# Gates of a graph layer: the two sums of a pair of units stand together, and the three parts of a pair are picked and passed through the sigmoid in another order

## What is computed

```python
hg = jnp.einsum('bnf,gf->bng', h3, Wg[:, :F])
qg = jnp.einsum('blf,gf->blg', q, Wg[:, F:]) + bg
attn = jax.nn.sigmoid(hg[:, :, None, :] + qg[:, None, :, :])
qi = jnp.einsum('bnlf,blf->bnf', attn, q)
```

## Time and profile before

| | |
|---|---|
| median of three runs | 1491.56 us (1490.84 to 1495.92) |
| span of the profiled execution | 1493.6 us |
| TensorE busy | 1374.3 us (92%) |
| VectorE busy | 992.7 us (66%) |
| ScalarE busy | 773.0 us (52%) |
| GpSimd busy | 225.7 us (15%) |
| pairs of the first gate | 155.3 to 275.1 us of the span |
| pairs of the second gate | 375.6 to 495.6 us |

### The profile page before, as it was taken

How to read it: one execution, slowest core, us unless ns; L and a number is a source line. 1 busy time by engine, 2 the same in 40 slices (tenths; PEclk the granted TensorE clock), 3 DMA queues, 4 the chain that set the end, 5 groups by cost and what they waited for, 6 DMA issues and landing times.

```text
span 1493.6 us, 24053 instructions
## 1 busy us (share of the span) xinstructions
PE 1374.3 (92%) x10000; PEld 1165.3 (78%) x10000; DVE 992.7 (66%) x1776; ACT 773.0 (52%) x1245; POOL 225.7 (15%) x115
## 2 busy tenths in 40 slices
PE   6999999999999798798789999888999999987998
PEld 5999633699533696588778899778899999976976
DVE  8655777745777756657667677776577767758355
ACT  2346788535788444344554454634345554436343
POOL 4201587100677100102001000001000000000100
PEclk8999999999999899999999899899899999988899
DMA  8174464135364222035324354063355555142100
GB/s 341 45 231 159 127 190 118 64 127 168 119 190 117 75 78 103 0 128 186 111 81 185 127 191 149 22 234 118 115 184 188 171 191 182 61 170 80 69 0 22
DMA packets 30834, 194.81 MB, mean 130 GB/s; under 512 B 4211, under 2 KB 4339, under 8 KB 14726
## 3 DMA queue, kind: packets, MB, share of 16 engines
q1 hardware_dynamic: 30726, 193.27, 38.1%
HBM read 183.03 MB, written 3.93 MB: 125 GB/s over the span
## 4 chain that ended last, share of the span: by engine, by line
PE 73%; DVE 15%; ACT 6%; POOL 3%; issue 1%; DMA 1%; SPq 0%; DVEq 0%; ACTq 0%; POOLq 0%
PE PS L357 58%; PE PS L956 6%; PE PS L965 5%; PE PS L362 3%; DVE WL L300 2%; POOL WK L1151 2%; PE PS L609 1%; PE PS L459 1%; POOL WL L307 1%; DVE SM L534 1%; ACT WH L293 1%; DVE SM L1323 1%; ACT WK L1708 1%; DVE WK L1733 1%; DVE WK L1738 1%
## 5 line engine op out<-in xcount | busy, mean ns | idle before, releaser
L300 DVE TENSOR_TENSOR WL<-w,WH 128x768 fp32r<-128x768 f32 x367 | 349.5, 963 | 216.1 <-ACT WH L293 213.5
L293 ACT ACTIVATE WH<-w 128x768 fp32r<-128x768 f32 x381 | 315.9, 841 | 272.3 <-PE PS L357 264.2
L357 PE MATMUL PS<-XS,WH 128*128 128x256 f32 x2292 | 418.5, 285 | 11.5 <-DVE XS L484 7.1
L357 PEld LDWEIGHTS PS<-XS,WH 128*128 128x128 f32 x2292 | 356.4, 190 | 15.7 <-issue 12.0
L357 PE MATMUL PS<-XS,WL 128*128 128x256 f32 x1146 | 324.2, 283 | 0.0
L357 PEld LDWEIGHTS PS<-XS,WL 128*128 128x128 f32 x1146 | 217.9, 190 | 0.0
L1089 DVE TENSOR_TENSOR WK<-PS,WK 128x1024 f32<-128x1024 f32 x128 | 156.7, 1224 | 55.6 <-ACT PS L1033 54.5
L1151 POOL TENSOR_TENSOR WK<-WK 128x1024 f32<-128x1024 f32 x64 | 152.8, 2392 | 205.7 <-ACT WK L1030 205.7
L357 PE MATMUL PS<-WH,GS 128*128 128x256 f32 x864 | 162.4, 286 | 6.8 <-DVE GS L484 6.7
L1033 ACT ACTIVATE PS<-PS 128x1024 f32<-128x1024 f32 x128 | 129.4, 1011 | 34.8 <-PE PS L956 34.8
L357 PEld LDWEIGHTS PS<-WH,GS 128*128 128x128 f32 x864 | 137.2, 192 | 9.7 <-DVE GS L484 8.1
(11 more groups left out here) (249 smaller groups left out, 2059.1 us busy)
## 6 DMA issues: line engine op xcount, KB each, us to landing
w<-f2W_in SPq DMA_DIRECT2D x40, 1152.0 KB, 5.5
w<-Wrel_in SPq DMA_DIRECT2D x12, 1152.0 KB, 9.0
WK<-qrep_in SPq DMA_DIRECT2D x16, 768.0 KB, 5.4
w<-f1Wi_in SPq DMA_DIRECT2D x8, 1152.0 KB, 5.9
w<-f1Wo_in SPq DMA_DIRECT2D x8, 1152.0 KB, 5.1
w<-f3Wqkv_in SPq DMA_DIRECT2D x6, 1152.0 KB, 13.8
RT<-qg_rows SPq DMA_DIRECT2D x16, 384.0 KB, 6.3
RT<-AS SPq DMA_DIRECT2D x32, 192.0 KB, 6.6
```

What stands on the lines that cost most here:

```text
L293: A.e.activation(w_hi(i), w_raw(i), ACT.Copy).then_inc(*hi("w", i))
L300: V.e.tensor_tensor(w_lo(i), w_raw(i), w_hi(i), ALU.subtract).then_inc(*lo("w", i))
L357: ins = T.e.matmul(o, l, r, start=i == 0 and first, stop=i == n - 1 and last, skip_group_check=lint)
```

## The change

In TensorE's loop the picks of a round are no longer those of one pair. A round p now has `select(p, 1)`, `select(p-1, 2)`, both sums of pair p-2, and then `select(p, 0)`; six picking matmuls stand in a row across the end of a round, then 16 summing ones (in the trace's count). `turn_q` stays the last thing of its round, which now puts it behind `select(p, 0)`. ScalarE takes the parts in the order 1, 0, 2. Nothing is added or taken away.

```diff
             T.wait_ge(act, "pick")
             gate_q(0)
             gate_q(1)
+            select(0, 1)
             select(0, 0)
-            select(0, 1)
             gate_q(2)
             select(0, 2)
             gate_q(3)
+            select(1, 1)
             select(1, 0)
-            select(1, 1)
             gate_q(4)
-            select(1, 2)
             gate_q(5)
             for p in range(2, NPR):
+                select(p, 1)
+                select(p - 1, 2)
+                sums(p - 2, 0)
+                sums(p - 2, 1)
                 select(p, 0)
-                select(p, 1)
-                sums(p - 2, 0)
-                select(p, 2)
-                sums(p - 2, 1)
                 if p % 4 == 2 and p > 4:
                     turn_q(p // 4 - 1)
+            select(NPR - 1, 2)
             for p in range(NPR - 2, NPR):
                 sums(p, 0)
                 sums(p, 1)
...
             feed_act(qh_ + 6)
             for p in range(NPR):
-                for q in range(3):
+                for q in (1, 0, 2):
                     attend(p, q)
```

## The result

| | before | changed |
|---|---|---|
| median | 1491.2 us (1488.4 to 1495.9, 4 runs) | 1510.45 us (1505.4 to 1517.5, 4 runs) |
| span of the profiled execution | 1493.6 us | 1505.4 us |
| first gate, first pick to the end of the last reduction | 119.8 us | 127.5 us |
| second gate | 120.0 us | 126.6 us |

The changed kernel is **slower by 1.1%** (ratio 1.0112, 95% interval 1.0078 to 1.0146), inside the range, on the side that was forecast, and somewhat more than the 1505 forecast. Executions of one kernel spread with their mean granted clock, in the seventeen runs of the kernel before beside e8 from 1487.9 us at 0.962 to 1502.9 us at 0.952, so what the change costs is read from stages of the profiles rather than from the two medians.

What follows compares the result with a forecast made beforehand. TensorE, busy for all of 70 us in mid-gate, was taken as the bound, with waits on other engines replacing it after the change. Per gate 0.2 + 1.45 + 2.9 + 2.1 = +6.65, two +13.3: median 1491.6 to 1505 us, range 1497 to 1511.

Steps and rivals of the forecast that it cites:

- Cost of the runs: TensorE's loop: six picks in one run 1.59 us, sixteen sums 1.42; 3.01 a pair, 0.35 less than before.
- Chain 1: Plain rounds: a part-1 pick waits for the previous pair's part-1 sigmoid, exposing its weights; 3.22 us a pair, low end 3.11.
- Chain 2: The turn waits for VectorE's copy behind the part-2 product, stalling TensorE by 0.72 us; the turn's pair takes 4.30.
- Chain 3: VectorE's reduction between the products of parts 0 and 2 delays a part-2 pick; that pair takes 3.58 us.
- A graph: Four pairs in a gate's loop take 14.32 us against 13.74: +0.58 each, +2.9 over five distances of turns.
- Up to the second turn: Start of a gate: +0.2 us in GpSimd's stretch and +1.45 for the turn's later place and stall.
- The tail: From the loop's last turn to the gate's end: 11.0 us against 8.91, so +2.1.
- The gate: Sum of the terms for one gate, 0.2 + 1.45 + 2.9 + 2.1 = +6.65 us; +13.3 for two.
- Late rows: Rival: rows of the next graph but one land late in some graphs; +1 to +4 us, 1507 to 1509; chance 0.12.
- the clock: Behind the gates: a longer tail can bring half clock to the first gate too or shift it; 1.7 us either way.
- The faster rival: TensorE stays the bound in the gates, copy ready within 2.74 us of the part-2 pick; 1483 us; chance 0.06.

Runs made afterwards that it cites:

- e8: The changed kernel unaltered, run again beside e5 to e7 on one chip; 1509.1 us, ratio 1.010 to the kernel before.
- e1: The changed kernel with the turn one round later, behind the sums and ahead of the pick of part 0; 1499.8 us, ratio 1.0047 to the kernel before.
- e2: e1 with VectorE's reduction also moved behind the product of part 2; 1497.9 us, ratio 1.0030 to the kernel before.
- e4: The changed kernel with the pick of part 0 between the two sums again; 1514.1 us in one run.
- e6: e5 with VectorE's reduction also moved behind the product of part 2; 1488.3 us, ratio 0.9952 to the kernel before.
- e3: The kernel before with only the sums joined behind picks 0, 1, 2 of a pair; 1500.6 us, ratio 1.0043 to the kernel before.
- e7: e6 with three useless matmuls before and three behind each gate's last turn; 1484.6 us in one run.
- e5: e3 with ScalarE taking the parts in the order 0, 2, 1; 1490.5 us in one run.

## Why the prediction was right, point by point

- **Cost of the runs.** Sixteen sums 1.42, as measured: 1.42. Six picks without a wait 1.59: every run of six in the changed kernel holds a wait, but e1 shows 217.71 - 216.13 = 1.58 behind a turn.
- **Chain 1, the sigmoid of part 1.** Forecast 3.22 to 3.23 us a round; measured 3.22 to 3.24 from one L1030 to the next in the plain rounds. The choice that a pick which waits in mid-run exposes its weights holds: its load starts when L1030 ends, and the rounds aren't 3.11. The Trainium skill (TensorE: Matmul & The Clock Gate, step-by-step) has weights pulled ahead of matmuls in flight; a load that itself has to wait isn't.
- **Chain 2, the turn.** Stall forecast 0.72, measured 0.73 and 0.74, before all seven turns that each gate has in its loop; the turn's round 4.30 forecast, 4.30 measured between two L1030 starts (227.89 and 232.19). e1 takes it away by moving the turn alone.
- **Chain 3, the reduction.** Forecast 3.58 for that round, measured 3.50, with the next at 3.28 instead of 3.22: the same sum. e2 takes it away.
- **A graph.** 14.32 forecast, 14.30 measured.
- **Up to the second turn.** +1.65 forecast (0.2 + 1.45); measured from the first pick +1.8 in the first gate and +1.7 in the second.
- **The tail.** 11.0 us from the loop's last turn to the end forecast; measured 284.63 - 273.32 = 11.3 in the first gate and 11.0 in the second. The first of these ran its last turn at half clock (0.90 us instead of 0.55).
- **The gate.** +6.65 forecast; measured +7.7 and +6.6, in e8 +6.6 and +7.1. The excess of the first is the row load below (0.65) and the last turn at half clock. In e8 the second gate has both (its last turn took 0.87 us, and one distance of turns was 14.47).
- **Late rows**, a rival with 0.12 on top of the forecast, came once with an effect in the profiled execution: 0.90 us before a pick, and the turns around it stand 14.95 apart instead of 14.30. A wait of 0.26 at 492.40 left its turns at 14.31.

```profile
261.21 0.74 PE L956 MATMUL PS<-RT,PK 128*128 128x512 f32 x2
262.85 1.20 PE L956 MATMUL PS<-RT,PK 128*128 128x512 f32 x4 [0.90 <-DMA RT<-AS]
```

- **What was undersized is the clock.** The prediction named it as 1.7 us either way and left it out of the sum. In the changed kernel (twice), e1, e2, e4 and e6 the stretch between the gates is 102.2 to 102.6 us, with the clock behind the first gate at 0.50 to 0.57; before, in e3 and in e7 it is 100.4 to 100.5, with the clock at 1.00; in e5 101.5, with 0.64. So the changed kernel pays 2.1 us behind its first gate. Behind the second the clock is at half before and after, so nothing is added there. With it the sum is 13.3 + 2.1 = 15.4, where the ratios of the two sets of runs, 1.0 and 1.1%, are 15 to 17 us. The forecast of 1505 and the median of 1510 differ by less than the changed kernel's own spread (1505 to 1517 in ten runs), so how near the one came to the other says little; the terms of the gates, each within 0.4 us once the late row is taken off, are what bears the forecast out.
- **The faster rival** failed where it said it would be decided: the pick of part 2 starts at 240.61 and the turn behind the copy at 244.06, 3.45 us later, not within 2.74. TensorE with no idle time and ScalarE 15% idle were true and didn't help. The Trainium skill's rule in TensorEngine Tiling (Key Properties), that a mode switch drains, is in line with the fixed cost of a run (0.21 and 0.14); halving the switches is worth 0.22 us a graph at the changed order (e4), since waits take its place.

## What to carry to other kernels

An engine that is busy for 100% of a stretch can still be one reordering away from being held by something else: before its queue is rearranged, each result it waits for should be followed link by link to its new due time, the rare ones (a copy once in four rounds) too, since a stall there holds up everything queued behind. The saving per round (0.35 us here) is an upper bound that a chain through another engine cuts (to 0.14), and once-a-graph waits can turn it over. The same grouping won 0.5% when the other engines' orders were changed with it: the part that the slow path needs first, the spare one last, and side work behind the product that is waited for.

## What the runs showed of the hardware that was not expected

- TensorE's clock in the 3.6 us behind a gate, after a tail in which TensorE idles in several pieces, was at half or full, and the length of the drain alone doesn't tell which. The kernel before drains alike in both gates (7.77 us between the last two turns) and had 1.00 behind the first and 0.53 behind the second; e4, with 9.57 between them in both, had 0.53 and then 1.00. Behind the first gate it was 0.50 to 0.64 in the changed kernel, e1, e2, e4, e5 and e6, and 1.00 in the kernel before, in e3 and, with idle matmuls in the tail, in e7. The price was about 2 us. What decides it stays open.
- A wait of TensorE on ScalarE in the middle of a run costs the wait and 0.1 us of weight load on top: the second pick of the run of 239.38 starts its load 0.67 us behind the first's, where both matmuls of a pick take 0.58, so the wait is 0.09; the run takes 1.79 where 1.59 was forecast without a wait, so 0.11 more are lost.
